# Destination logits of a graph attention kernel: one fp32 product a visit in place of three bf16 products in two bursts a group

## The reference, cut to what matters

```python
z  = (x @ W).reshape(N, num_heads, head_dim)
el = jnp.sum(z * attn_l, axis=-1)
er = jnp.sum(z * attn_r, axis=-1)
e  = leaky_relu(el[src] + er[dst], 0.2)
ex = jnp.exp(e - segment_max(e, dst)[dst])
alpha = ex / segment_sum(ex, dst)[dst]
out = segment_sum(alpha[:, :, None] * z[src], dst) + z + bias
```

## Time and profile before

| | us |
|---|---|
| median of 3 runs | 2788.51 (2784.93 to 2790.27) |
| the profiled execution's own time | 2792.58 |
| its span (first to last instruction) | 2790.9 |
| PE busy | 2546.9 (91%) |
| DVE busy | 2158.4 (77%) |
| POOL busy | 1488.1 (53%) |
| ACT busy | 1242.0 (45%) |
| mean granted TensorE clock | 0.967 of full speed |

### The profile page before, as it was taken

One profiled execution on the slowest core, in us unless ns is written; L12 is line 12 of the kernel. 1 busy time (PEld: TensorE's weight loads), 2 busy tenths in 40 slices (PEclk: granted clock), 3 DMA queues, 4 the chain that ended last, 5 costly groups with the idle time before them and its releaser, 6 DMA issues.

```text
span 2790.9 us, 53062 instructions
## 1 busy us (share of the span) xinstructions
PE 2546.9 (91%) x13226; PEld 1800.2 (65%) x13229; DVE 2158.4 (77%) x4457; ACT 1242.0 (45%) x2607; POOL 1488.1 (53%) x1528
## 2 busy tenths in 40 slices
PE   2997999999999979999999999799999998679998
PEld 1886666666668866666666688556565555467776
DVE  6776999999997769999999977577776776853332
ACT  1223666666654435666666544233333335511111
POOL 1003777777722147777777312477777772124443
PEclk9998999999999989999999999899999999879999
DMA  6445999999958889999999687899999999967776
GB/s 213 165 169 198 336 345 348 339 340 331 333 202 211 216 215 326 346 342 335 345 345 337 216 221 210 231 334 333 337 325 338 334 340 342 358 131 145 145 146 117
DMA packets 199342, 763.41 MB, mean 274 GB/s; under 512 B 41889, under 2 KB 58033, under 8 KB 198542
## 3 DMA queue, kind: packets, MB, share of 16 engines
q0 software_dynamic: 127632, 604.14, 66.3%
q1 hardware_dynamic: 53790, 108.21, 12.8%
q10 hardware_dynamic: 17760, 48.79, 4.4%
HBM read 640.01 MB, written 133.45 MB: 277 GB/s over the span
## 4 chain that ended last, share of the span: by engine, by line
PE 51%; DVE 21%; issue 8%; DMA 7%; POOL 6%; ACT 4%; SPq 2%; ACTq 1%; DVEq 1%; POOLq 0%
PE PS L1065 28%; DVE arena L1512 6%; PE PS L984 6%; PE PS L1188 5%; POOL arena L677 4%; PE PS L1177 4%; DMA arena<-table,src_k 4%; PE PS L986 3%; DVE parts L1530 2%; SPq L498 2%; PE PS L1161 1%; DVE arena L1349 1%; DVE arena L1381 1%; DVE arena L1371 1%; DVE arena L1370 1%
## 5 line engine op out<-in xcount | busy, mean ns | idle before, releaser
L677 POOL DMA_INDIRECT arena<-table,src_k x945 | 943.6, 998 | 309.1 <-issue 191.0
L1065 PE MATMUL PS<-arena,S 128*128 128x384 f32 (+1 forms) x1848 | 676.3, 500 | 4.6 <-DVE arena L1512 4.6
L1512 DVE TENSOR_TENSOR arena<-arena,PS 128x768 f32<-128x768 f32 x630 | 580.8, 947 | 0.9 <-ACT arena L827 0.9
L1065 PEld LDWEIGHTS PS<-arena,S 128*128 128x128 f32 x1848 | 341.8, 191 | 180.6 <-issue 14.5
L1065 PE MATMUL PS<-parts,S 128*128 128x384 f32 (+2 forms) x1332 | 332.3, 371 | 54.1 <-DVE parts L1530 28.7
L677 POOL DMA_INDIRECT W<-table,src_k x300 | 294.9, 983 | 92.6 <-issue 74.6
L623 POOL DMA_DIRECT2D table<-arena x75 | 41.5, 554 | 564.5 <-DVEq L1393 388.3
L1065 PE MATMUL PS<-arena,S_weighted 128*128 128x384 f32 (+1 forms) x840 | 307.7, 508 | 18.1 <-DVE S_weighted L1518 18.1
L1065 PEld LDWEIGHTS PS<-parts,S 128*128 128x128 f32 x1332 | 221.5, 189 | 97.2 <-issue 84.3
L835 ACT ACTIVATE apart<-iota_row,dst_k 128x128 f32<-128x128 f32 x830 | 260.3, 389 | 19.7 <-issue 9.1
L786 ACT ACTIVATE parts<-arena 128x780 fp32r<-128x780 f32 x168 | 142.6, 851 | 248.4 <-DVE arena L1512 240.5
(11 more groups left out here) (295 smaller groups left out, 4530.2 us busy)
## 6 DMA issues: line engine op xcount, KB each, us to landing
arena<-mixed SPq DMA_DIRECT2D x63, 384.0 KB, 3.6
table<-arena POOLq DMA_DIRECT2D x50, 396.0 KB, 3.2
local_b<-local SPq DMA_DIRECT2D x123, 160.0 KB
mixed<-sums ACTq DMA_DIRECT2D x50, 384.0 KB
arena<-table SPq DMA_DIRECT2D x50, 384.0 KB, 4.7
arena<-table,src_k POOLq DMA_INDIRECT x945, 5.7
table<-arena POOLq DMA_DIRECT2D x25, 384.5 KB, 4.6
out<-last_bias POOLq DMA_DIRECT2D x25, 384.0 KB, 6.3
```

Of the source, the lines that this page charges most:

```text
L677: nc.gpsimd.indirect_dma_start(edge_row(l, k % U)[:, 0:table_width(l)], None, table[l][:, :], bass.IndirectOffsetOnAxis(src_k[:, k:k + 1]. ...
L1065: o = nc.tensor.matmul(flat[:, bass.ds(bank + 512 * c, n)], onehot, row[:, c * HALF:c * HALF + n], start=False, stop=True, skip_group_chec ...
L1512: nc.vector.tensor_tensor(z, z, a, ALU.mult).then_inc(s_msg, 1)
```

## The change

The three bf16 parts and `erp` go. The turned one-hot is written as fp32 straight into `ST`, and each visit has one plain fp32 product with `erm`, in all three layers. It is issued behind the sums of each visit, so five times a group, three groups ahead as before. With one head DVE reads both numbers from PSUM, without `destination`, and the four remaining steps lie at visits 1, 2, 3 and 3 of the group. `local_b` has a place of its own (it shared `ST`'s), and the gates' parts, which lay in `erp`, have one too.

```diff
-        erp = sb("erp", [P, NB * 3 * 2 * HMAX], BF16)
+        with nc.sbuf_tensor("gate_part", [P, 3 * TOP * NB], BF16) as gate_part:
+            pass
+        local_b = sb("local_b", [P, NBUF, G * P], U8)
...
-        with nc.sbuf_tensor("local_b", [P, NBUF, G * P], U8) as local_b:
-            with nc.sbuf_tensor("ST_b", [P, NBUF, G * P], BF16) as ST_b:
-                pass
         ST = sb("ST", [P, NBUF, G, P])
...
-                    if H == 1:
-                        o = nc.tensor.matmul(er_parts(jj)[:, j, :], ST_b[:, jj, j * P:(j + 1) * P],
-                                             erp[:, bass.ds(b * 6, 6)], start=True, stop=True)
-                    for part in range(3 if H > 1 else 0):
-                        o = nc.tensor.matmul(er_of(l, jj)[:, j, :], ST_b[:, jj, j * P:(j + 1) * P],
-                                             erp[:, bass.ds(b * (6 * H) + part * 2 * H, 2 * H)],
-                                             start=(part == 0), stop=(part == 2))
+                    o = nc.tensor.matmul(er_of(l, jj)[:, j, :], ST[:, jj, j, :],
+                                         erm_flat(l)[:, bass.ds(b * (2 * H), 2 * H)], start=True, stop=True)
...
                         add_up(g, j, words[j])
-                        if j in (1, 3) and g + ER_LEAD < NG:
-                            for n in ((0, 1), (2, 3, 4))[j // 2]:
-                                er_of_edges(g + ER_LEAD, n, later(words[n]))
+                        if g + ER_LEAD < NG:
+                            er_of_edges(g + ER_LEAD, j, later(words[j]))
...
-                part = [erp[:, 0:NB * 6 * H].rearrange("p (b j h) -> p b j h", b=NB, j=3)[:, :, j, :] for j in range(3)]
-                link(nc.vector.tensor_copy(part[0], e3))
-                link(nc.vector.tensor_tensor(e3, e3, part[0], ALU.subtract))
-                link(nc.vector.tensor_copy(part[1], e3))
-                nc.vector.tensor_tensor(part[2], e3, part[1], ALU.subtract).then_inc(s_erm, 1)
...
-                    nc.vector.tensor_scalar(ST_b[:, jj, :], local_b[:, jj, :], own_code[:, 0:1], None,
+                    nc.vector.tensor_scalar(ST[:, jj, :, :].rearrange("p g e -> p (g e)"), local_b[:, jj, :], own_code[:, 0:1], None,
                                             ALU.is_equal).then_inc(s_ST, 1)
...
-                    def destination():
-                        dve.wait_ge(s_er, g + (NG * l + 1))
-                        dc.mark(nc.vector.tensor_reduce(both, er_parts(jj).rearrange("p g (t h) -> p g h t", t=3), AX_X, ALU.add))
-
                     def logits():
-                        dc.follow()
+                        dve.wait_ge(s_er, g + (NG * l + 1))
...
-                        dc.mark(nc.vector.tensor_tensor(u, edge_heads(l, jj), both[:, :, 0:1], ALU.add))
+                        dc.mark(nc.vector.tensor_tensor(u, edge_heads(l, jj), er[:, :, 0:1], ALU.add))
...
-                        dc.mark(nc.vector.tensor_tensor(u, u, both[:, :, 1:2], ALU.subtract))
+                        dc.mark(nc.vector.tensor_tensor(u, u, er[:, :, 1:2], ALU.subtract))
...
-                        if steps and H == 1 and j <= 3:
-                            steps[j]()
+                        if steps and H == 1 and 1 <= j <= 3:
+                            steps[j - 1]()
                         if steps and H == 1 and j == 3:
-                            steps[4]()
+                            steps[3]()
```

More of the change, by code:

```diff
@@ L330, in er_of @@
             return group_bank(jj)[:, 0:G * 2 * HEADS[l]].rearrange("p (g h) -> p g h", g=G)
-        def er_parts(jj):
-            return group_bank(jj)[:, 0:G * 6].rearrange("p (g h) -> p g h", g=G)
         def columns(jj):
@@ L446, in gate_parts @@
         def gate_parts():
-            return erp[:, 0:3 * TOP * NB].rearrange("p (w j b) -> p w j b", w=3, j=TOP)
+            return gate_part[:, :].rearrange("p (w j b) -> p w j b", w=3, j=TOP)
         def logits_turned(b):
@@ L1441, in node_sweep @@
                     link(nc.vector.scalar_tensor_tensor(out=second, in0=ert3, scalar=SLOPE, in1=first, op0=ALU.mult, op1=ALU.add))
-                    link(nc.vector.tensor_tensor(first, ert3, first, ALU.add))
+                    nc.vector.tensor_tensor(first, ert3, first, ALU.add).then_inc(s_erm, 1)
                 else:
@@ L1445, in node_sweep @@
                     link(nc.vector.tensor_tensor(ert3, ert3, highest, ALU.add))
-                    link(nc.vector.scalar_tensor_tensor(out=second, in0=ert3, scalar=SLOPE, in1=ert3, op0=ALU.mult, op1=ALU.max))
-                part = [erp[:, 0:NB * 6 * H].rearrange("p (b j h) -> p b j h", b=NB, j=3)[:, :, j, :] for j in range(3)]
-                link(nc.vector.tensor_copy(part[0], e3))
-                link(nc.vector.tensor_tensor(e3, e3, part[0], ALU.subtract))
-                link(nc.vector.tensor_copy(part[1], e3))
-                nc.vector.tensor_tensor(part[2], e3, part[1], ALU.subtract).then_inc(s_erm, 1)
+                    nc.vector.scalar_tensor_tensor(out=second, in0=ert3, scalar=SLOPE, in1=ert3,
+                                                   op0=ALU.mult, op1=ALU.max).then_inc(s_erm, 1)
             def edge_sweep(l):
@@ L1465, in exponents, with logits @@
                     t, u = wt[:, jj, :, 0:H], wu[:, :, 0:H]
-                    both = wu[:, :, 2:4]
-                    def destination():
+                    def logits():
                         dve.wait_ge(s_er, g + (NG * l + 1))
-                        dc.mark(nc.vector.tensor_reduce(both, er_parts(jj).rearrange("p g (t h) -> p g h t", t=3), AX_X, ALU.add))
-                    def logits():
-                        dc.follow()
                         for j in range(jj * G, (jj + 1) * G):
                             dve.wait_ge(s_z[j], 16 * i + 16 * (uses(jj) * l + 1))
-                        dc.mark(nc.vector.tensor_tensor(u, edge_heads(l, jj), both[:, :, 0:1], ALU.add))
+                        dc.mark(nc.vector.tensor_tensor(u, edge_heads(l, jj), er[:, :, 0:1], ALU.add))
                     def leaky():
@@ L1503, in exponents @@
                         return both_logits, higher
-                    return destination, logits, leaky, less_bound, limit
+                    return logits, leaky, less_bound, limit
                 def message(g, i, jj, j):
@@ L1595, in edge_sweep @@
                 with dve.Fori(1, NI - 2) as i:
-                    dc.enter(i - 1, (1 if H > 1 else 4) * NBUF)
+                    dc.enter(i - 1, (1 if H > 1 else 3) * NBUF)
                     body(i)
```

## The result

| | before | changed |
|---|---|---|
| median of 4 runs, us | 2788.32 (2784.93 to 2790.27) | 2854.64 (2851.31 to 2860.09) |
| profiled execution: own time, span | 2792.58, 2790.9 | 2851.49, 2849.9 |
| ratio of the times | | 1.0241, 95% interval 1.0219 to 1.0263 |

The forecast was 2862 us in a range of 2830 to 2897. The medians lie 66 us apart, the two profiled executions 59: the profile of before is one of the slower executions of its kernel, the one of the changed kernel one of its fastest.

A forecast was written before the change was run, and what follows sets the result against it. TensorE was to bound all three edge sweeps (chance 0.75): +24.5, +26.4 and +22.4 make 73.3 us, on the median of 2788.5 giving 2862 us, range 2830 to 2897.

The forecast's parts named there:

- TensorE's slack: Edge sweeps before: TensorE's spare time, 1.3 us a turn (27 us a sweep) in the first two, 2.4 (51) in the third.
- a chain through TensorE: Rival, all edge sweeps: waits run through TensorE itself, extra work adds in full, 147 us, 2936; chance 0.10 for above +105.
- The price of the product: Each visit on TensorE: two bare fp32 weight loads, 2 x 0.109 = 0.218 us.
- The estimate in which nothing overlaps: Each visit on TensorE, by the Trainium skill's rule: three bare loads, 0.327 us, some 45 us more a sweep.
- the one at 0.08 us a pass: Rival, each visit: a product costs 0.162 us, a turn 26.4, some 2795 us; chance 0.08 for this and all up to +40.
- The terms kept for waits: TensorE waits remaining in the edge sweeps: 5, 5 and 8 us, from ranges 0 to 22 and, in the third, 0 to 47.
- The turn: 20 visits of the loop on TensorE: 27.56 us in the first two sweeps, 26.7 in the third.
- The half clock at the start: Start of each edge sweep: TensorE at 1.2 instead of 2.4 GHz for 11.5 us, losing 4.5 us.
- the +5 us bound: DVE, first sweep: if the wider fp32 one-hot cost half as much again, some +5 us a sweep more at worst.
- `destination`'s going: DVE: `destination`, 179 ns a group, goes; TensorE won't wait for it, so nothing gained.
- The later `s_er`: Edge sweeps: a group's products end after visit 4 instead of 3, `s_er` comes one visit later, costing nothing.
- Ahead of a sweep: Before the first sums: four DVE instructions go, 7 us, but first logits wait for gathered rows, so 0.

The follow-up runs named there:

- three kernels with the loads where they were: Kernel before with: bf16 products behind each visit, 2798.55 us; one bf16 burst a group, 2784.23 us; fp32 products behind each visit in third layer alone, 2805.41 us.
- the other three with early loads and no long gather: Kernel before with first turned one-hots ahead of erm, 2785.73 us; that plus one burst a group, 2782.39 us; changed kernel with fp32r products, 2781.38 us.
- one pass: Changed kernel with `ST` and `erm` as fp32r, so the destination product has one pass with one weight load: 2781.38 us, ratio to before 0.9972.

## Why the prediction was right, by its own steps

**What bounds the kernel.** TensorE's slack was reckoned at 1.3 us a turn in the first two sweeps and 2.4 in the third, and TensorE was to become the bound of all three. It did: chains of 96 to 100% on TensorE's two lines, and a doubled product that adds in full. That the waits of before were for a DVE that gives way, not a chain through TensorE, is shown by their going: for split rows from 14.2 us to 4.9 in the first sweep, from 24 to none in the third. The chain of the second sweep, 71% TensorE's, was the one put forward for it; that of the first had only 17% on TensorE's sums. Where two engines are nearly even, the share of the chain is a weak witness, and the sum of an engine's own work against the length of a turn was the better one.

**The price of the product.** 0.218 us reckoned, from loads of products of 12 and of 128 columns; 0.22 in the timeline, 0.225 from the doubled product. The trace had no such product before, but every part of it: a load that hides under 0.33 us of streaming, and two that don't. The estimate in which nothing overlaps, 0.327 us, and the one at 0.08 us a pass, 0.162, both fall.

**The sweeps.** The terms kept for waits were 5, 5 and 8 us; measured 4.9, 4.9 and 0. The two 5s were taken out of a range of 0 to 22 without a row that gives them, so that they hit is luck. The turn was reckoned at 27.56 us and is 27.65 (the 20 visits from 505.54 to 533.19 us), 2 us a sweep. The half clock at the start was put at 4.5 us in each sweep. In the changed kernel the granted clock is 0.90 from 261.5 to 277.0 us, 0.91 from 1053.3 to 1070.0 and 0.68 from 1835.8 to 1850.0, and full behind. A clock of 0.90 over 15.5 us is 3.1 us at 1.2 instead of 2.4 GHz, which lose 1.5 us; the second start loses 1.5 as well, the third 4.5. So in the first two sweeps this term was 3 us too high and the turn 2 us too low, and 578.1 is met to the tenth partly because they cancel. In the third the waits are the mis-sized term: 8 us kept, none measured, against 2 us more for a turn of 26.8 (14 x 1.515 + 6 x 0.93), which makes the 6 us by which its forecast was high. I had argued that GpSimd, at 25 us a turn, would be near the new rate and make up late gathers slowly; but its 25 us against 26.8 left it enough, and in the sweep's own waits a late gather reached DVE (19 us) and never TensorE.

**DVE.** The wider one-hots cost nothing: the changed kernel's L1445 has a median of 548 ns, and L1459 had 553. So the +5 us bound was not needed. `destination`'s going was hidden, as said.

**Order.** The later `s_er` was to cost nothing. In the third sweep DVE waits 42 us for it; TensorE doesn't. Right in time, wrong in that no wait was foreseen.

**Ahead of a sweep** was put at 0, and is where a mechanism was missed. The first sums come at 261.52 instead of 264.14. I had seen that the gathers hold the start, and concluded that earlier products change nothing; but `turned` also frees the buffers for the next loads of codes, and in the kernel before these were in flight beside the fifth gather. I had written that on SP's queue nothing moves. It moved 3.6 us. How much of the 2.6 us that makes is open, since three kernels with the loads where they were have their first sums at 262.1 to 262.5 us. Counted from the last instruction that makes `erm` ahead of its parts (L1442, changed L1432) to the first sums it is 16.5 us before and 15.3 to 16.2 in those three, 14.0 in the changed kernel and 14.6 to 14.9 in the other three with early loads and no long gather: a gain, of some 1 to 2 us.

From the last sums of a sweep to the first of the next, two times, it is 2.8 and 3.2 us less. Part of that lies where the sweep hands over to the next node sweep, TensorE's first transposes after the sums, before and changed, first hand-over:

```profile
822.14 1.51 PE L969 MATMUL PS<-ident,arena 128*128 128x128 f32 x6 [4.40 <-issue]
```

```profile
842.46 0.85 PE L965 MATMUL PS<-ident,arena 128*128 128x128 f32 x6 [2.84 <-issue]
```

TensorE idles 1.6 us less there (1.9 less at the second, 3.27 to 1.40). That DVE, which prepares these rows, has got ahead of TensorE by the sweep's end is the likely reason, and the experiments fit it: with products twice as dear the two gaps are 1.56 and 1.19 us, and with one pass, the changed kernel's order but no longer TensorE's bound, 4.59 and 4.70. What DVE does in these gaps was not followed. The transposes run at full clock (0.85 us for six, 1.51 before), but that isn't the change's doing: with fp32 in bursts they took 1.51 us at the same place, with one burst of bf16 0.85.

In the profiles the forecast was 2866 us and 2851.5 came, 14.4 less: 6.4 in the sweeps and 8 elsewhere. The medians miss by 7 us only, since the profile of before lies 4.1 us above the median that the forecast took, and that of the changed kernel 3.2 below its own. So the close hit on the medians is in part luck, and the sweeps' 6 us, nearly all of it the third's waits, is the miss that stands clear.

## What to carry to other kernels

A narrow fp32 product costs TensorE its weight loads, not its columns: 0.22 us with 24 columns and with 2. Count the bare loads, those with nothing long streaming above them: one for each pass here, and plain fp32 has two passes. Where three bf16 products in a burst stream at 26 ns each, one fp32 product at 0.22 us is dearer though it is one instruction in the code.

When an engine gets work on top, look whose waits it eats. Waits for an engine that is only as full as itself mostly vanish (14.2 us to 4.9 here); the forecast is then the engine's own sum plus the start and a few us.

An instruction moved earlier also moves what its completion releases on other queues: follow each semaphore to the DMAs behind it before a move is put down at nothing.

## What the runs showed of the hardware that I had not expected

In the kernels with fp32 products in bursts and with doubled products, GpSimd's second gather of the first sweep took 5.82 us where it takes 0.97 to 1.28 in the other kernels, with first sums at 264.8 and 263.8 us instead of 261.5. The row of the first of them:

```profile
249.03 5.82 POOL L673 DMA_INDIRECT arena<-table,src_k  x1 [0.30 <-issue]
```

In the changed kernel the same one takes 0.98 us. What holds it was not tried; it costs 2 to 3 us once, and it is part of the measured spans of these two.
